# A four-layer graph network on one core: outputs and inverses kept in PSUM, inverses laid out by GpSimd for a one-pass spread, and a new order of work

## The reference

```python
# layer 0: attention with 8 heads of 32, weighted by adj, projection, layer norm
logits = q @ k.T / sqrt(32) + log(clip(adj, 1e-8))
x1 = layer_norm(x + softmax(logits) @ v @ Wo.T + bo)
# layer 1 (and layer 3 with other weights): graph attention of one head
p = x1 @ fc_w.T + fc_b;  logits = p @ q_w.T + q_b + (p @ k_w.T + k_b).T
m = logits + (1 - adj) * -1e9;  m = where(m >= 0, m, 0.01 * m)
x2 = softmax(m) @ p + x1
# layer 2: attention with 8 heads, weighted by adj, with a gate term for each row and column
scores = Q @ K.T / sqrt(32) + (x2 @ w_g[:256])[:, None] + (x2 @ w_g[256:])[None, :] + b_g + log(adj + 1e-9)
x3 = softmax(scores) @ V + x2
```

## Time and profile before

| | |
|---|---|
| median of three runs | 1846.9 us (1844.34 to 1847.38) |
| the profiled execution | 1851.17 us, its span 1849.3 us |
| instructions in it | 68980 |
| TensorE busy | 1777.7 us, 96% |
| VectorE busy | 1597.8 us, 86% |
| ScalarE busy | 1318.2 us, 71% |
| GpSimd busy | 670.2 us, 36% |
| mean granted clock of TensorE | 0.984 of full |

### The profile page before, as it was taken

One profiled execution on the slowest core, in us unless ns is written; L12 is line 12 of the kernel. 1 busy time (PEld: TensorE's weight loads), 2 busy tenths in 40 slices (PEclk: granted clock), 3 DMA queues, 4 the chain that ended last, 5 costly groups with the idle time before them and its releaser, 6 DMA issues.

```text
span 1849.3 us, 68980 instructions
## 1 busy us (share of the span) xinstructions
PE 1777.7 (96%) x28388; PEld 1679.8 (91%) x28388; DVE 1597.8 (86%) x3486; ACT 1318.2 (71%) x3536; POOL 670.2 (36%) x731
## 2 busy tenths in 40 slices
PE   5899999999999999999999999999999999999985
PEld 5799999999999999999999999999999999999985
DVE  4589889889889889889889889889889889888884
ACT  3577777777777777777777777777777777777763
POOL 2234344344344244244334334334334334334321
PEclk7899999999999999999999999999999999999997
DMA  3010111111111111011011011011011011011000
GB/s 114 19 37 29 44 48 34 40 48 35 38 48 39 34 48 43 30 48 47 26 48 47 26 48 47 25 48 48 25 48 48 25 48 48 25 48 48 25 22 18
DMA packets 48260, 74.57 MB, mean 40 GB/s; under 512 B 5456, under 2 KB 21968, under 8 KB 47952
## 3 DMA queue, kind: packets, MB, share of 16 engines
q1 hardware_dynamic: 47376, 69.49, 11.9%
q10 hardware_dynamic: 576, 0.68, 0.1%
HBM read 53.37 MB, written 16.78 MB: 38 GB/s over the span
## 4 chain that ended last, share of the span: by engine, by line
PE 71%; DVE 21%; issue 6%; ACT 1%; DMA 0%; POOL 0%; DVEq 0%; SPq 0%; POOLq 0%; ACTq 0%
PE banks L870 12%; PE banks L923 12%; PE banks L871 9%; PE banks L872 9%; PE banks L967 7%; PE banks L1062 6%; PE banks L958 6%; DVE xt_lo L650 6%; DVE weights_B L779 5%; DVE logits L723 3%; PE banks L973 3%; DVE logits L719 2%; PE banks L1056 2%; PE banks L1050 2%; PE banks L1022 2%
## 5 line engine op out<-in xcount | busy, mean ns | idle before, releaser
L431 POOL TENSOR_TENSOR xb_t<-sum_t,cols_tile 128x512 f32<-128x512 f32 x128 | 133.2, 1041 | 307.8 <-DVE sum_t L741 301.2
L478 POOL TENSOR_TENSOR weights_A<-weights_A,adj 128x512 f32<-128x512 f32 x64 | 82.5, 1289 | 407.4 <-ACT weights_A L548 407.4
L456 POOL TENSOR_TENSOR xt_lo<-x_t,xt_hi 128x512 fp32r<-128x512 f32 x64 | 82.4, 1288 | 317.1 <-ACT xt_hi L581 317.1
L630 ACT ACTIVATE logits<-logits,f_inv 128x128 f32<-128x128 f32 x256 | 89.0, 395 | 151.2 <-DVE f_inv L840 151.2
L755 DVE TENSOR_REDUCE least_cols_A<-banks 128x4 f32<-128x512 f32 x256 | 169.7, 685 | 15.3 <-PE banks L923 15.2
L779 DVE TENSOR_TENSOR weights_A<-banks,adj 128x512 f32<-128x512 f32 x192 | 132.4, 692 | 52.6 <-ACT banks L548 49.1
L870 PE MATMUL banks<-w_hi_v,xt_hi 128*128 128x258 f32 (+1 forms) x512 | 154.3, 301 | 13.0 <-DVE w_lo_v L650 9.8
L870 PE MATMUL banks<-w_hi_f,xt_hi 128*128 128x258 f32 x512 | 164.0, 320 | 0.8 <-DVE xt_lo L650 0.8
L755 DVE TENSOR_REDUCE least_B<-banks 128x4 f32<-128x512 f32 x256 | 163.9, 682 | 0.9 <-PE banks L932 0.9
L623 ACT ACTIVATE logits<-logits,f_neg_max 128x128 f32<-128x128 f32 x256 | 102.2, 411 | 85.7 <-DVE f_neg_max L726 85.7
L650 DVE TENSOR_TENSOR xt_lo<-sum_t,xt_hi 128x512 fp32r<-128x512 f32 x128 | 154.0, 1203 | 9.3 <-ACT xt_hi L581 2.1
(11 more groups left out here) (181 smaller groups left out, 6210.1 us busy)
## 6 DMA issues: line engine op xcount, KB each, us to landing
x_t<-x_t_dram SPq DMA_DIRECT2D x64, 256.0 KB, 3.6
x_in<-x_dram SPq DMA_DIRECT2D x64, 256.0 KB, 3.8
out_dram<-x_out SPq DMA_DIRECT2D x64, 256.0 KB, 2.4
adj_t<-adj_t_dram SPq DMA_DIRECT2D x64, 128.0 KB, 3.4
adj<-adj_dram SPq DMA_DIRECT2D x64, 128.0 KB, 2.0
scratch<-weights_dram SPq DMA_DIRECT2D x9, 256.0 KB, 7.0
scratch<-weights_dram ACTq DMA_DIRECT2D x2, 256.0 KB, 4.2
out_bias<-L_gnn_bo_dram ACTq DMA_DIRECT2D x1, 128.0 KB, 7.5
```

The costliest lines, as they stand in the source:

```text
L431: return pool.tensor_tensor(result, x, col_tile.unsqueeze(2).broadcast_to([P, KT, GROUP * P]), ALU.add)
```

## The change

- The denominators' reciprocal stays in its PSUM bank. DVE's rounded part and low part are taken from there, into a tile inv_both. POOL then has a new step `den`, which multiplies inv_both by a constant mask `own` into four blocks of inv_parts (128x512). `wide` is one matmul of 512 columns with one stationary matrix, and waits for POOL's semaphore inv_placed instead of DVE's inv_split.
- The product of heads and inverses is written back to the PSUM bank of `wide`, where ACT (high part), DVE (low part) and `sum` read it. That bank is therefore held until ot_lo_ready (A) or x3_ready (B).
- The bias of layer 2 is no longer added by POOL. It is carried: folded into layer 3's bias and into a column out_col that `bias` 3 adds. `sum` takes x2 itself, in a tile sum_t_2 that now has two buffers.
- `ac` leaves DVE. ACT makes `soul` (the row term) and c_cols behind its second v2 copy, and the exponentials take the column term straight from v_B.
- In the setup the output bias is made ahead of the first scores (`bias_of_outputs`), in bank 3, and POOL's first `bias` 0 waits for that alone.
- All lists of ORDER are new. The diff's core (of ORDER only its head; line numbers of the new file differ):

```diff
 ORDER = {
     "tensor": [
...
-        inv_den = {s: sb(f"inv_den_{s}", [P, P]) for s in "AB"}
         inv_hi = {s: sb(f"inv_hi_{s}", [P, P], F32R) for s in "AB"}
-        inv_parts = {s: sb(f"inv_parts_{s}", [P, P], F32R) for s in "AB"}
-        ot = {s: sb(f"ot_{s}", [P, GROUP, DIM]) for s in "AB"}
+        inv_both = {s: sb(f"inv_both_{s}", [P, P]) for s in "AB"}
+        inv_parts = {s: sb(f"inv_parts_{s}", [P, UNITS, P], F32R) for s in "AB"}
...
-        spread = sb("spread", [P, UNITS, HALF, HEAD_DIM], F32R)
+        spread = sb("spread", [P, HALF, HEAD_DIM], F32R)
+        own_all = sb("own_all", [P, UNITS, HALF, HEAD_DIM // UNITS])
+        own = sb("own", [P, UNITS])
...
             if name == "den":
-                return inverted[where], g + 1
+                return inv_split[where], g + 1
             if name == "wide":
-                return ot_ready[where], g + 1
+                return (ot_lo_ready if where == "A" else x3_ready), g + 1
...
                         if G.no == 0:
-                            pool.wait_ge(setup_dve, SETUP_DONE)
+                            pool.wait_ge(setup_dve, dve_step["out_bias", "", ""])
                             pool.wait_ge(cols_landed, 16)
                         pool.wait_ge(x_landed, 16 * (G.no + 1))
                         G.wait_former(pool, summed, GROUP, 2)
                         pool.tensor_tensor(x_0[:, G.odd, :, :], x_in[:, :, :],
                                            out_bias[:, :].unsqueeze(1).broadcast_to([P, GROUP, DIM]), ALU.add
                                            ).then_inc(x_biased["0"], 1)
-                    elif name == "bias" and where in ("2", "3"):
-                        if where == "2":
-                            pool.wait_ge(x2_ready, G.no + 1)
-                            G.wait_former(pool, x3_ready, 1, 2)
-                        else:
-                            pool.wait_ge(x3_ready, G.no + 1)
-                            G.wait_former(pool, out_ready, 1, 2)
-                        add_col(xb_t[where][:, G.odd, :, :], sum_t[where][:, :, :], row_bias[where]
-                                ).then_inc(x_biased[where], 1)
+                    elif name == "bias" and where == "3":
+                        pool.wait_ge(x3_ready, G.no + 1)
+                        G.wait_former(pool, out_ready, 1, 2)
+                        pool.tensor_tensor(xb_t["3"][:, G.odd, :, :], sum_t["3"][:, 0, :, :],
+                                           out_col[:, :].unsqueeze(2).broadcast_to([P, KT, GROUP * P]), ALU.add
...
+                    elif name == "den":
+                        if G.no == 0:
+                            pool.wait_ge(setup_dve, dve_step["own", "", ""])
+                        pool.wait_ge(inv_split[where], G.no + 1)
+                        pool.tensor_tensor(inv_parts[where][:, :, :],
+                                           inv_both[where][:, :].unsqueeze(1).broadcast_to([P, UNITS, P]),
+                                           own[:, :].unsqueeze(2).broadcast_to([P, UNITS, P]), ALU.mult
+                                           ).then_inc(inv_placed[where], 1)
...
-                            act.wait_ge(ac_ready, G.no + 1)
+                            act.wait_ge(v_ready["B"], GROUP * (G.no + 1))
                             for g in range(GROUP):
                                 last = act.activation(to[:, cols(g, 2 * P)], x[:, cols(g, 2 * P)], ACT.Exp,
-                                                      bias=ac[:, G.odd, g, 1:2], scale=-1.0)
+                                                      bias=v["B"][:, G.odd, g, DIM + 1:WIDE], scale=-1.0)
...
-                        act.activation(ot_hi[:, :, :], ot["A"][:, :, :], ACT.Copy).then_inc(ot_hi_ready, 1)
+                        act.activation(ot_hi[:, :, :].rearrange("p g d -> p (g d)"), bank[BANK["wide", "A", 0]], ACT.Copy).then_inc(ot_hi_ready, 1)
...
+                            if n == GROUP - 1:
+                                act.wait_ge(v_ready["B"], GROUP * (G.no + 1))
+                                G.wait_former(act, least_ready["B"], 1, 2)
+                                act.activation(soul[:, G.odd, :], v["B"][:, G.odd, :, DIM], ACT.Identity,
+                                               bias=soul_b[:, 0:1]).then_inc(soul_ready, 1)
+                                act.activation(c_cols[:, :, 0:GROUP], v["B"][:, G.odd, :, DIM + 1].unsqueeze(1).broadcast_to(
+                                    [P, HALF, GROUP]), ACT.Copy).then_inc(c_cols_ready, 1)
...
-                dve.wait_ge(row_landed, 16)
-                dve.tensor_tensor(out_bias[:, :], product("out_bias", 0), out_bias[:, :], ALU.add).then_inc(setup_dve, 1)
...
                 if (name, where, n) == ("max", "A", 0):
                     low_parts(FIRST)
+                    dve.wait_ge(row_landed, 16)
+                    dve.wait_ge(products_made, product_done["out_bias", 0])
+                    dve.tensor_tensor(out_bias[:, :], product("out_bias", 0), out_bias[:, :], ALU.add
+                                      ).then_inc(setup_dve, 1)
                     low_parts(SECOND)
...
-                        dve.reciprocal(inv_den[where][:, :], bank[b][:, 0:P]).then_inc(inverted[where], 1)
+                        dve.reciprocal(bank[b][:, 0:P], bank[b][:, 0:P]).then_inc(inverted[where], 1)
                         dve.wait_ge(inverted[where], G.no + 1)
-                        dve.tensor_copy(inv_hi[where][:, :], inv_den[where][:, :]).then_inc(inv_rounded[where], 1)
+                        dve.tensor_copy(inv_hi[where][:, :], bank[b][:, 0:P]).then_inc(inv_rounded[where], 1)
                         dve.wait_ge(inv_rounded[where], G.no + 1)
-                        dve.scalar_tensor_tensor(inv_parts[where][:, :], inv_den[where][:, :], low_row[:, :],
+                        dve.scalar_tensor_tensor(inv_both[where][:, :], bank[b][:, 0:P], low_row[:, :],
                                                  inv_hi[where][:, :].bitcast(F32), ALU.mult, ALU.subtract
                                                  ).then_inc(inv_split[where], 1)
                     elif name == "wide":
...
-                        dve.tensor_tensor(ot[where][:, :, :].rearrange("p g d -> p (g d)"), bank[b],
+                        dve.tensor_tensor(bank[b], bank[b],
                                           heads[where][:, :, :].rearrange("p g d -> p (g d)"), ALU.mult
                                           ).then_inc(ot_ready[where], 1)
                     elif name == "sum":
                         dve.wait_ge(ot_ready["B"], G.no + 1)
-                        dve.wait_ge(x_biased["2"], G.no + 1)
+                        dve.wait_ge(x2_ready, G.no + 1)
                         G.wait_former(dve, x_biased["3"], 1, 1)
-                        dve.tensor_tensor(sum_t["3"][:, :, :].rearrange("p k (g n) -> p k g n", g=GROUP),
-                                          ot["B"][:, :, :].rearrange("p g (k n) -> p k g n", k=KT),
-                                          xb_t["2"][:, G.odd, :, :].rearrange("p k (g n) -> p k g n", g=GROUP), ALU.add
+                        dve.tensor_tensor(sum_t["3"][:, 0, :, :].rearrange("p k (g n) -> p k g n", g=GROUP),
+                                          bank[BANK["wide", "B", 0]].rearrange("p (g k n) -> p k g n", g=GROUP, k=KT),
+                                          sum_t["2"][:, G.odd, :, :].rearrange("p k (g n) -> p k g n", g=GROUP), ALU.add
                                           ).then_inc(x3_ready, 1)
...
-                        low_part(ot_lo[:, :, :], ot["A"][:, :, :], ot_hi[:, :, :]).then_inc(ot_lo_ready, 1)
+                        low_part(ot_lo[:, :, :].rearrange("p g d -> p (g d)"), bank[BANK["wide", "A", 0]],
+                                 ot_hi[:, :, :].rearrange("p g d -> p (g d)")).then_inc(ot_lo_ready, 1)
...
-                    elif name == "ac":
-                        dve.wait_ge(v_ready["B"], GROUP * (G.no + 1))
-                        dve.tensor_tensor(ac[:, G.odd, :, :], v["B"][:, G.odd, :, DIM:WIDE],
-                                          soul_b[:, :].unsqueeze(1).broadcast_to([P, GROUP, 2]), ALU.add
-                                          ).then_inc(ac_ready, 1)
-                        dve.wait_ge(ac_ready, G.no + 1)
-                        dve.tensor_copy(c_cols[:, :, 0:GROUP], ac[:, G.odd, :, 1].unsqueeze(1).broadcast_to(
-                            [P, HALF, GROUP])).then_inc(c_cols_ready, 1)
...
+            def bias_of_outputs():
+                pe.wait_ge(cols_landed, 16)
+                pe.wait_ge(raw_landed["o0"], 16)
+                for j in range(KT):
+                    last = pe.matmul(product("out_bias", 0), bv_col[:, j:j + 1].broadcast_to([P, P]), raw["o0"][:, j, :],
+                                     start=(j == 0), stop=(j == KT - 1))
+                last.then_inc(products_made, 1)
+                pe.wait_ge(setup_dve, dve_step["out_bias", "", ""])
...
```

(10 more changed lines are left out.)

105 lines of the change are left out of this document (59 added, 46 removed), and 42 rows, old and new, of the table ORDER.

## The result

The changed kernel takes 1875.3 us (median of four runs, 1873.55 to 1876.91) where the kernel before, run beside it, takes 1846.8. The ratio is 1.0157, with a 95% interval of 1.0139 to 1.0174. It was predicted at 1812 us, range 1796 to 1840, faster with a chance of 0.86. It is slower, outside the range, and on the side to which the prediction gave 0.10.

What follows compares the result with a forecast made beforehand. The prediction took the loop to be bound by PE, busy 96% of the span, with a fill and a drain. Its terms, -25 - 10 - 1 + 1 = -35 us, applied to the median of 1846.9, gave 1812 us, range 1796 to 1840.

Steps and rivals of the forecast that it cites:

- -25, -10, -1 and +1: Forecast terms in us: one-pass spread with its part in fill and drain, new order's waits, fill, drain; sum -35.
- the walk of leg B: Score banks from B's shift to den B: PE work 3.8 us, ACT and DVE 4.0, so PE waits 0.1 to 0.2.
- leg A: Score banks, scores A to den A: PE 10.2 us, DVE 8.8, or 9.9 if xt_lo3 meets GpSimd; PE waits 0 to 0.3.
- Rival 1: The waits stay: both legs' waits add up to 0.4 us or more a turn; 1822 to 1838 us, chance 0.27.
- The one-pass spread: PE's spread of inverses as one 512-column matmul, 0.24 to 0.26 us each; gain 0.40 us a turn, 24 us in 61.
- the slow start: Slower matmul right behind each spread, 0.17 us instead of 0.12 to 0.13; one of two a turn was expected to remain.
- The placing: GpSimd's new 128x512 step between split and spread, 1.29 us each; hidden for A, for B hidden by 0.5 us.
- Rival 2: Placing comes late, PE waits 1.3 to 1.8 us at spread B; 1880 us at 1.3; chance 0.11 with any other slower order.
- DVE: VectorE's work: two gate operations go (0.3 us a turn), edited operations add 0.1, so lighter by 0.2 a turn.
- its lateness at single places is: Claim that DVE's total busy time, 179.3 of 200 us, is no bound, but its coming late at single places is.
- Fill: Start of run: earlier output bias saves 2.6 us, low parts and setup work stand against it; -1 us, bounds -4 and +4.
- Drain: End of run: last placing is in the open, +1.3 us less what the shorter order saves; +1 us.

Runs made afterwards that it cites:

- b1: Changed kernel with layer 3's mask earlier on PE and GpSimd's penalty step ahead of its weighing of B, nothing left out: 1818.3 us, ratio 0.9837 against the kernel before.

## Why the prediction was wrong

**The sum by its own steps**, for the profiled execution of 1873.2 us against 1849.3. PE's own work fell by 0.28 us a turn (27.92 less the 1.01 of the turn shown, against 27.55 less 0.36), -17 us over 61 turns. The waits went from 0.36 to 1.01, +40. The fill was 1.7 us shorter, the drain 3.1 longer. Together +24, as measured. Predicted were -25, -10, -1 and +1.

**The step that failed is the walk of leg B**, from B's shift to `den` B. It counted for DVE "the last weighing, 0.69 with two handoffs of 0.1", and came to a wait of 0.1 to 0.2 us. It took for granted that DVE is at the weighings in time. On DVE's list layer 3's mask stands ahead of them (0.6 for the masked logits, 0.42 leaky, 0.42 maximum), and that is a further chain, from PE's mask transposes over DVE to the weighings, in parallel with ACT's exponentials. Without a block it would still have been in time: the leaky step's 1.05 us of waiting is the whole of the 1.01, and in b1, where the step meets nobody, `den` B waits 0.1 us a turn, as the walk had it. The prediction looked for a meeting with GpSimd on leg A (xt_lo3, which took 0.69 us and met nobody) and named low parts alone as suspects. The leaky step has two SBUF inputs as well. The trace before had a sign of it: a mean of 630 ns over a shortest of 424 and a longest of 851. The Trainium skill (SBUF — State Buffer, "Who interferes with whom") states that issue order, not the shape of an operation, decides who is blocked. The trace agrees: issued 0.1 us behind GpSimd's weighing the step loses 1.05 us, issued 0.4 us ahead of it (b1) nothing, and 128x2 is blocked like 128x256. The prediction held the rule in its hand and applied it to the low parts and the sum, and not to the leaky step.

**Rival 1** (the waits stay) was the right mechanism, underpriced. It said that one block costs 1.06 us and that leg B has no slack, and then bounded the two legs together by 0.66. By its own numbers one block on leg B is a wait of about 1.06 + 0.15: (1.21 - 0.36) x 61 = +52 on the -25 that it kept, or 1874 us. The range would have had to reach there.

**The one-pass spread** was right in its price: 0.25 us was forecast for the instruction behind, and 0.26 (after), 0.25 and 0.24 (b1) were measured. The gain was put at 0.40 and is 0.35 a turn in b1's order. PE's own work fell by only 0.28 in the changed kernel, so the new order gave some 0.07 back. The rows show one place where that much went: the transposes of x1 take 0.47 us up to the next instruction behind the spread,

```profile
914.05 0.39 PE L1002 MATMUL banks<-inv_parts_B,spread 128*128 128x512 f32 x1
914.31 0.63 PE L1052 MATMUL banks<-ident,x 128*128 128x128 f32 x4
914.78 1.06 PE L1092 MATMUL banks<-fpt,fp 128*128 128x128 f32 x8
```

where they took 0.36 ahead of it (907.12 in the earlier trace rows to 907.48 in the earlier trace rows). The kernel with four pieces in b1's order spends 0.39 us at the spread of B, not the 0.47 of the earlier trace rows, and 0.46 at these transposes. So it was the order, and not the one pass, that took the slow start off the spread of B, and it put one onto the transposes instead; the prediction had counted it as saved.

**The placing** was hidden, as forecast. It takes 1.04 us, not 1.29, and PE waits 0.9 us behind it in the whole run for B and 0.3 for A. Rival 2, which ended on the right side, had the wrong mechanism. **DVE** became lighter by 0.3 us a turn (174.58 x 27.92 / 200 = 24.4, against 24.7), with the block at the leaky step about equal to the one that went; 0.2 was forecast. That DVE got lighter and the kernel slower bears out that "its lateness at single places is" the bound. **Fill**: `den` A of group 0 starts at 39.94 instead of 37.81, so the earlier output bias did not bring it forward; yet the scores of group 2 come 1.7 us earlier. **Drain**: PE waits 0.67 us behind the last placing, and from the last scores of A on the mean granted clock was 0.83 instead of 0.88.

**Not settled**: which of the list's many moves the fill's 1.7 us and the drain's 3.1 come from, and the shorter ends of the kernel with four pieces and of the one with GpSimd's small weighing.
